# A wait between the second and the third gather of a supertile in the first layer of a graph network

## The reference

```python
def layer0(x, src, dst, edge_attr, W1, b1, W2, b2, Wg, bg, gamma, beta):
    ei = concatenate([x[src], edge_attr], axis=-1)          # 100000 edges, 256 + 64 wide
    core = maximum(ei @ W1 + b1, 0.0) @ W2 + b2
    gate = sigmoid(ei @ Wg + bg)
    agg = segment_sum(gate * core, dst, num_segments=3125)
    return layernorm(agg + x) * gamma + beta

def layer1(h, Wf, Wb, loop_weight, ..., src, dst, etypes):
    # forward: for each edge (h @ Wf[etype])[src] + bias, divided by the in-degree, summed over dst
    # backward: the same with Wb, src and dst exchanged
    return 2 * (h @ loop_weight) + self_bias + m_forward + m_backward

x = x + layer0(relu(layernorm(x)), src, dst, edge_attr, ...)
x = x + layer1(relu(layernorm(x)), ..., src, dst, edge_type)
```

## Time and profile before

| | us |
|---|---|
| median of 3 runs | 4423.52 (4414.99 to 4432.65) |
| the profiled execution | 4418.46 |
| its span, first to last instruction | 4416.7 |
| PE busy | 3478.9 |
| DVE busy | 2476.3 |
| POOL busy | 2308.7 |
| first layer's loop | about 76 to 1585 |

### The profile page before, as it was taken

One profiled execution on the slowest core, in us unless ns is written; L12 is line 12 of the kernel. 1 busy time (PEld: TensorE's weight loads), 2 busy tenths in 40 slices (PEclk: granted clock), 3 DMA queues, 4 the chain that ended last, 5 costly groups with the idle time before them and its releaser, 6 DMA issues.

```text
span 4416.7 us, 72963 instructions
## 1 busy us (share of the span) xinstructions
PE 3478.9 (79%) x21136; PEld 2939.8 (67%) x21137; DVE 2476.3 (56%) x3465; ACT 1007.0 (23%) x1734; POOL 2308.7 (52%) x2362
## 2 busy tenths in 40 slices
PE   6999999999999979976666676767657766777776
PEld 5888888888888858864554555555445555665555
DVE  6888887888788888854554532222323333333334
ACT  3444444444444444410110110010100000000000
POOL 1555555555555500036555666656566655666663
PEclk8999999999999989988888888888867878888878
DMA  4555555555555525544443464444333322233332
GB/s 165 157 159 155 157 156 152 157 155 159 149 152 154 157 81 205 204 131 124 132 129 118 132 141 134 126 129 132 111 92 87 89 82 80 85 89 88 90 88 79
DMA packets 322746, 569.91 MB, mean 129 GB/s; under 512 B 73897, under 2 KB 218393, under 8 KB 322585
## 3 DMA queue, kind: packets, MB, share of 16 engines
q0 software_dynamic: 137984, 411.19, 33.2%
q1 hardware_dynamic: 182732, 154.33, 10.6%
q10 hardware_dynamic: 1868, 2.52, 0.2%
HBM read 452.43 MB, written 115.41 MB: 129 GB/s over the span
## 4 chain that ended last, share of the span: by engine, by line
PE 52%; issue 17%; DVE 12%; another core or an unknown queue 12%; DVEq 6%; ACT 1%; ACTq 0%; DMA 0%; POOL 0%; SPq 0%; POOLq 0%
PE pc L697 13%; PE pa L706 11%; PE pu L687 4%; PE pu L745 4%; PE pg L671 4%; PE pa L745 4%; PE pg L745 4%; DVE key L1249 3%; DVE tops L1246 3%; PE pu L679 3%; DVEq L277 1%; PE pu L800 1%; PE pc L659 1%; DVE onehot L1023 1%
## 5 line engine op out<-in xcount | busy, mean ns | idle before, releaser
L428 POOL DMA_INDIRECT fa<-proj,gslot x784 | 744.8, 950 | 865.6 <-issue 569.8
L416 POOL DMA_INDIRECT fa<-ptab,slot x784 | 814.2, 1039 | 721.8 <-issue 375.1
L440 POOL DMA_INDIRECT hr<-proj,gslot x784 | 745.8, 951 | 446.7 <-issue 226.3
L706 PE MATMUL pa<-fa,onehot 128*128 128x258 f32 x1760 | 517.1, 446 | 363.0 <-DVE onehot L1023 196.5
L706 PEld LDWEIGHTS pa<-fa,onehot 128*128 128x128 f32 x1760 | 379.7, 222 | 480.1 <-issue 374.8
L697 PE MATMUL pc<-ws,hr 128*128 128x256 f32 x4704 | 649.2, 290 | 43.2 <-issue 40.5
L697 PEld LDWEIGHTS pc<-ws,hr 128*128 128x128 f32 x4704 | 598.3, 193 | 64.5 <-issue 61.7
L745 PE MATMUL pu<-hr,fa 128*128 128x258 f32 x1056 | 295.6, 425 | 132.6 <-issue 129.2
L1056 DVE TENSOR_TENSOR acc<-acc,pa 128x258 f32 x196 | 82.7, 422 | 503.4 <-remote 303.8
L745 PEld LDWEIGHTS pu<-hr,fa 128*128 128x128 f32 x1056 | 225.2, 214 | 194.2 <-issue 157.5
L745 PE MATMUL pg<-hr,fa 128*128 128x258 f32 x1040 | 278.8, 417 | 74.5 <-issue 72.0
(11 more groups left out here) (153 smaller groups left out, 5048.8 us busy)
## 6 DMA issues: line engine op xcount, KB each, us to landing
proj<-fa SPq DMA_DIRECT2D x400, 256.0 KB
fa<-in_ea_t SPq DMA_DIRECT2D x196, 128.0 KB
fa<-ptab,slot POOLq DMA_INDIRECT x784
fa<-proj,gslot POOLq DMA_INDIRECT x784
hr<-proj,gslot POOLq DMA_INDIRECT x784
fa<-in_Wrel SPq DMA_DIRECT2D x32, 256.0 KB
ptab<-fa SPq DMA_DIRECT2D x25, 256.0 KB, 2.0
out<-res SPq DMA_DIRECT2D x4, 768.0 KB
```

What stands on the lines that cost most here:

```text
L416: pool.indirect_dma_start(pbuf[:, n % 2, j, :], None, ptab[:, :], bass.IndirectOffsetOnAxis(ap=slot[:, n, j:j + 1], axis=0)).then_inc(s_ga ...
L428: pool.indirect_dma_start(gbuf[:, n, j, 0:H], None, proj[0][:, :], bass.IndirectOffsetOnAxis(ap=gslot[:, at, j:j + 1], axis=0)).then_inc(s ...
L440: pool.indirect_dma_start(raw2[:, n, j, 0:H], None, proj[1][:, :], bass.IndirectOffsetOnAxis(ap=gslot2[:, n, j:j + 1], axis=0)).then_inc(s ...
L706: last = nc.tensor.matmul(pa[:, bank, 0:width], keys[:, at, j, :], rows[:, j, :], start=(n == 0), stop=(n == len(todo) - 1))
```

## The change

Between the second and the third gather of a supertile GpSimd waits until VectorE has signalled the messages of supertile s-3 (`s_msg` reaches s-2), and increments `s_go` behind the wait. The four gathers, their semaphores and everything on the other engines stay as they are.

```diff
--- before.py
+++ after.py
@@ -413,6 +413,9 @@
                 pool.wait_ge(s_plan, GS // 2 * rnd + n // 2 + 1)
                 pool.sem_inc(s_go, 1)
                 for j in range(J):
+                    if j == J // 2 and past(s, 3):
+                        pool.wait_ge(s_msg, s - 2)
+                        pool.sem_inc(s_go, 1)
                     pool.indirect_dma_start(pbuf[:, n % 2, j, :], None, ptab[:, :],
                                             bass.IndirectOffsetOnAxis(ap=slot[:, n, j:j + 1], axis=0)
                                             ).then_inc(s_gath[0][n % 2], 16)
```

## The result

The first comparison gave 4376.97 us in the median for the changed kernel (4366.22 to 4383.47, four runs) against 4420.71 us (4414.99 to 4432.65, four runs): ratio 0.9895, 95% interval 0.9865 to 0.9925. That is 44 us less, where 70 was forecast. The experiments then showed that this isn't so everywhere: on three chips (3, 2 and 12) the kernel before takes 3766 us, and on the two of them on which the changed kernel was timed (3 and 2) it takes the same time.

What follows compares the result with a forecast made beforehand. TensorE was taken to bound the first layer's loop, held back by unbroken gather bursts. 4418.5 us - 70 + 0 + 0 = 4348.5, put at 4353 us because this execution is 5 us under the median; range 4325 to 4465.

Steps and rivals of the forecast that it cites:

- What bounds the kernel: First layer's loop: TensorE, 94% busy, sets the pace; unbroken bursts of four gathers hold back its signal and part of its work.
- Nothing for the added instructions: GpSimd, first layer: one wait and one increment for each of 193 supertiles cost 0, as GpSimd is idle 46%.
- The pause: Before the third gather: the wait delays it 0.5 us in the mean; always there if signals aren't held.
- What the pause gives: Second product (L697) of the first layer: back to 3.12 us from 3.53 gains at most 78 us; 90%, 70 us, taken.
- Delays at 0: Gathers queued behind the wait: 0.5 to 1.0 us later against 2.2 us in hand before the transposes, so 0 us.
- Rival 1: First layer: coupling is chance, or so short a pause doesn't break a burst; 4423 us, 4402 to 4445, chance 0.21.
- Rival 2: First layer: second gather pair holds TensorE's signal, closing a loop of 7.7 us a turn; 4478 us, 4445 to 4510, chance 0.22.
- What would show it: Trace signs in the first layer: longer idle before third gathers, prompt ScalarE starts, whole second product, loop 60 to 75 us shorter.

Runs made afterwards that it cites:

- older wait: Changed kernel with GpSimd's wait moved to the messages one supertile further back, so the pause goes and the two instructions stay: 4350.24 us, 0.9996 on chip 7.
- one-hot wait: Changed kernel with GpSimd waiting for VectorE's one-hot matrix, finished 0.75 us later, instead of the messages: 4274.77 us, 0.983 on chip 7; 3770.25 us, 1.0009 without hold.
- landing wait: Kernel before, with GpSimd waiting before each third gather until the supertile's first gather has landed: 4343.73 us, ratio 0.9986 on chip 7.

## Why the prediction was right, and where it was not

*What bounds the kernel.* Right for the chip of its trace. TensorE's lost time beside unbroken bursts was the gathers' doing: half of them gone, it is gone (ratio 0.9725); with the wait so old that it makes no pause, it stays (0.9996), and with a longer pause most of it goes (0.983), all on chip 7. I had written "This is the pattern, not a chance", which held; what I took for granted was that it belongs to the kernel. On three chips it isn't there. The prediction also has the signal held "until the burst is over"; it came 1 us later than that (810.41, the fourth gather's issue over at 809.36).

*Nothing for the added instructions.* Right: with the older wait they cost nothing that can be told from zero (0.9985 to 1.0007).

*The pause: "mean 0.5 us, nothing in 38% of them, 0.5 or more in 41%".* That was worked out from the old rhythm and came out nearly so: 71 of 189 third gathers without one, 42% with 0.5 or more. What failed is the sentence behind it, "If signals aren't held, bursts start early, [...] and the pause is always there, 0.5 us or more". Passed signals were followed by late bursts (the one at 267.00 came behind a ScalarE start at 263.44, 0.12 us after the transposes), since the burst waits for VectorE's gate sum and VectorE still carried the lateness of the supertile before. And in the loop without hold (the changed kernel on chip 3) the median pause was 0.3 us, where the estimate for the quick rhythm had 0.55 from the earlier trace rows.

*What the pause gives: 78 bound, 70 taken.* The mechanism was right and this term is the one that was mis-sized. The recovered part is 33 us by the rows above, 44 by the median. I had counted every pause as a passed signal; but only those from 0.65 us on let it through, 72 bursts, and the 40 shorter ones were all held. The bound was mis-sized as well, the other way. It prices the second product alone, and the whole hold was twice that: 155 us of the first chip's loop (1500 against 1345), so the change gave back a fifth of it. That the 70 isn't further from the 44 measured is in part luck, two errors that work against each other. The one-hot wait gives a long enough pause in most supertiles and gained 78 us, but on chip 7, where the same working as for the bound gives some 50 us and the whole hold is 119: the two 78s agree by chance.

*Delays at 0, with 2.2 us in hand.* Nearly right. The lowest tenth of the times between landing and transposes fell from 1.7 to 0.8 us, by the last landing on record. And bursts whose third gather was stretched, so that the fourth started 2 us or more after it, rose from 14 to 22; the supertile behind such a one takes 9.15 us in the mean against 7.22 for the others. Eight more at 1.9 us are some 15 us, an estimate. It is an upper one: stretched fourth gathers fell at the same time from 8 to 1, and no run shows that the stretch is what makes those supertiles long.

*Rival 1, no change.* Its time for this chip was wrong. The Trainium skill's rule, "SBUF — State Buffer", section "Who interferes with whom", that TensorE and ScalarE wait for nobody and DMAs don't contend with engines, agrees with the traces at 3766 us and disagrees with those at 4352 and 4421 us; at 4352 us the gathers cost the first layer's loop 119 us.

*Rival 2, the closed loop.* Not seen in the changed kernel. The kernel with the landing wait may show its germ: signals behind a late second pair come late, and the gain of the first kind is eaten; that the second pair holds them was only argued.

*What would show it.* Idle 0.8 us or more before the third gather in most supertiles (a spacing of 1.75): no, in 42%. ScalarE within 0.3 us in most: 36% instead of 22%. Product at 3.1 to 3.2 us: 77% of them, the mean 3.33. Its idle time well under 43 us: 24.6. Distance of transposes 6.7 to 7.0: 7.44 instead of 7.59, though 94 supertiles instead of 45 ran at under 6.75. Loop 60 to 75 us shorter: 33.

## What to carry to other kernels

A disturbance that works by threshold has to be removed by a margin: sort the events of the trace by the length of the pause and see where the hold ends, before taking a share of the bound. And take the bound from everything that runs late, not from the one product in which the idle time is plain to see. Tie the pause to an event that comes late enough even when the rhythm has quickened, since the cure changes the rhythm from which it was measured. And look at a stall that no semaphore explains on a second chip before tuning against it: there it may not exist, and the cure is then only a delay.

## What the runs showed of the hardware that was not expected

The same program with the same transfers (569.91 MB in some 322,700 packets, and VectorE's and ScalarE's instructions of the same durations) took 4421 us in the first comparison, 4352 us on chip 7 and 3766 us on chips 3, 2 and 12. Between 120 and 1400 us the granted clock was 0.99 and 1.00 on both kinds (first chip, chip 3), so it isn't the clock that parts them in the first layer. But the first layer has only 119 of the 586 us between chips 7 and 3. Behind it the clock differs too; the stretch from 2000 to 2500 us, first chip and then chip 3 (the clock is the third number from the end):

```profile
2000.00:2500.00 500.00, 330.81 (x1219) 258.55 (x1220) 260.61 (x447) 48.73 (x83) 295.27 (x311) 0.85 0.43 127
```
```profile
2000.00:2500.00 500.00, 399.85 (x1619) 313.42 (x1620) 248.98 (x445) 64.64 (x108) 378.57 (x399) 0.96 0.59 166
```

The page's sums for the second layer's products and the addition that waits for them, first on chip 3, without hold; the same lines on the first chip are below it:

```profile
L706 PE MATMUL pa<-fa,onehot 128*128 128x258 f32 x1760 | 448.2, 400 | 193.8 <-issue 81.9
L1056 DVE TENSOR_TENSOR acc<-acc,pa 128x258 f32 x196 | 82.6, 421 | 328.1 <-PE pa L706 326.5
```
```profile
L706 PE MATMUL pa<-fa,onehot 128*128 128x258 f32 x1760 | 517.1, 446 | 363.0 <-DVE onehot L1023 196.5
L1056 DVE TENSOR_TENSOR acc<-acc,pa 128x258 f32 x196 | 82.7, 422 | 503.4 <-remote 303.8
```

The unnamed releases are the mark of the hold: 303.8 us of them in the one trace, and in the other TensorE is named for 326.5 of 328.1. The products' 446 ns instead of 400 can be the lower clock as well as the hold, and no run parts them. In the third layer, where gathers follow each other for longer, TensorE could be seen to advance in single steps beside them (one-hot wait, chip 7):

```profile
3300.52 0.95 POOL L443 DMA_INDIRECT hr<-proj,gslot  x1 [0.30 <-issue]
3300.85 0.38 PE L748 MATMUL pu<-hr,fa 128*128 128x258 f32 x1 [0.41 <-issue]
3301.55 0.19 PEld L748 LDWEIGHTS pu<-hr,fa 128*128 128x128 f32 x1 [1.31 <-issue]
3301.78 0.95 POOL L443 DMA_INDIRECT hr<-proj,gslot  x1 [0.31 <-issue]
3302.26 0.38 PE L748 MATMUL pu<-hr,fa 128*128 128x258 f32 x1 [1.03 <-issue]
```

By the kernel these matmuls wait for nothing. The gathers start 1.26 us apart and the matmuls 1.41 us, with the weight load 0.70 us behind the one and 0.71 us ahead of the other.

The two kinds of trace differ in one thing more. The profile keeps records of the increments of semaphores. The first layer's 784 gathers make 16 each, on two semaphores, 6272 on either. The trace of the kernel before has 6254 and 6140 of them on chip 3, but 2836 and 3499 on the first chip, while it has every instruction on both (72,963). All six traces from the first chip and chip 7 have such holes; in the eight others at most a few per cent are missing. In the kernel with half of the gathers, on chip 7, the loop has no hold and nearly no hole (3112 and 3145 of 3168); in the kernel with the one-hot wait, where most signals pass, the holes stay (3029 and 4476 of 6272). So wherever gathers hold TensorE, records are missing too. All times here are of executions of which a span and a clock are on record; whether there is a hold where nothing is recorded was not tried. That writing the records takes part in the hold is a rival that nothing here rules out, and with it the change might gain less, or nothing, outside the profiler.

What makes the difference, whether it is the chip, something that ran beside it at the time, or the recording, and by what way a gather's issue reaches TensorE, stays open. Each chip was used in one group of runs, so chip and time can't be told apart.
